# Routing stage of a two-layer block: unread products on TensorE, a merge in four column groups, exponentials kept in PSUM

## The reference, cut to what matters

```python
logits = jnp.einsum('bsd,ed->bse', x, gate_w) + gate_b      # x: 8 x 512 x 256, 32 experts
probs = jax.nn.softmax(logits, axis=-2)                      # over the 512 tokens
vals_t, idx_t = jax.lax.top_k(probs.transpose(0, 2, 1), K)   # K = 8
...
tok = jnp.take_along_axis(x, flat_idx[:, :, None], axis=1)
tok = tok.reshape(b, K, E, d)
merged = jnp.einsum('bked,bke->bed', tok, vals)              # 8 x 32 x 256
```

## Time and profile before

| | us |
|---|---|
| median of three runs | 1335.1 |
| the three runs | 1330.59, 1335.10, 1335.44 |
| the profiled execution | 1329.41 |
| its span in the trace | 1327.7 |
| PE busy | 1281.6 |
| DVE busy | 1050.0 |
| ACT busy | 948.6 |

### The profile page before, as it was taken

The page is one execution under the profiler, slowest core; times in us unless marked ns, Lnnn a source line. Parts: engine busy times, 40 slices in busy tenths (PEclk is TensorE's granted clock), DMA queues, the critical chain, the costliest instruction groups (busy, mean ns, idle before and its releaser), DMA issues. The chain is left out here.

```text
span 1327.7 us, 32264 instructions
## 1 busy us (share of the span) xinstructions
PE 1281.6 (97%) x11493; PEld 1068.5 (80%) x11493; DVE 1050.0 (79%) x3340; ACT 948.6 (71%) x2384; POOL 318.5 (24%) x694
## 2 busy tenths in 40 slices
PE   4799999999999999999999999999999789999999
PEld 3587788888878888888879788887978578888888
DVE  6968896989689689868986897798689757767673
ACT  5869895988589588858885986788598724444333
POOL 4533331322133222212331223133133100000000
PEclk9999999999999999999999999999999999999999
DMA  6552231323223232323323232233223222222100
GB/s 212 200 159 89 90 127 59 120 104 101 78 94 121 74 105 74 126 69 103 128 75 104 75 129 86 82 97 106 89 89 112 78 77 63 57 57 56 57 17 33
DMA packets 90831, 125.18 MB, mean 94 GB/s; under 512 B 8760, under 2 KB 77104, under 8 KB 90672
## 3 DMA queue, kind: packets, MB, share of 16 engines
q1 hardware_dynamic: 90352, 123.11, 28.6%
q10 hardware_dynamic: 320, 0.00, 0.0%
HBM read 103.69 MB, written 19.40 MB: 93 GB/s over the span
## 5 line engine op out<-in xcount | busy, mean ns | idle before, releaser
L1213 ACT ACTIVATE prob<-prob,low 128x512 f32<-128x512 f32 (+3 forms) x512 | 281.2, 552 | 107.1 <-DVE low L1376 107.1
L1376 DVE CUSTOM_DVE_ANT_0 prob<-at,mask 128x512 f32<-128x512 f32 (+3 forms) x512 | 219.7, 485 | 8.9 <-PE at L960 8.9
L947 PE MATMUL at<-w_hi,c_lo 128*128 128x386 f32 x512 | 187.9, 367 | 0.8 <-DVE area_raw L1321 0.8
L947 PE MATMUL at<-w_lo,c_hi 128*128 128x386 f32 x512 | 174.1, 340 | 0.0
L947 PE MATMUL at<-w_hi,c_hi 128*128 128x386 f32 x512 | 173.9, 340 | 0.0
L1389 DVE TENSOR_SCALAR prob<-prob,rec 128x512 f32<-128x512 f32 (+3 forms) x512 | 169.9, 395 | 4.5
L999 PE MATMUL at<-ident,prob 128*128 128x128 f32 x1280 | 165.9, 276 | 4.5 <-DVE low L1376 1.8
L1027 PE MATMUL at<-probT,v 128*32 128x512 f32 (+3 forms) x2048 | 152.7, 439 | 2.6 <-DVE probT L1399 2.6
L999 PEld LDWEIGHTS at<-ident,prob 128*128 128x128 f32 x1280 | 141.8, 140 | 14.8 <-issue 4.6
L1527 POOL TENSOR_TENSOR area_sq<-area_sq 128x512 f32<-128x512 f32 x64 | 82.3, 1287 | 249.7 <-ACT area_sq L1177 249.7
L1027 PEld LDWEIGHTS at<-probT,v 128*32 128x32 f32 x2048 | 60.7, 110 | 93.4 <-issue 82.5
(11 more groups left out here) (265 smaller groups left out, 3226.8 us busy)
## 6 DMA issues: line engine op xcount, KB each, us to landing
area_w<-in_L_ffn_w SPq DMA_DIRECT2D x65, 1024.0 KB, 5.6
bias<-in_L_ffn_w SPq DMA_DIRECT2D x160, 32.0 KB, 4.4
x_in<-in_L_attn_x SPq DMA_DIRECT2D x8, 512.0 KB, 5.5
xr<-in_L_attn_x SPq DMA_DIRECT2D x8, 512.0 KB, 4.7
eo_d<-hidT SPq DMA_DIRECT2D x32, 128.0 KB, 1.8
x_d<-xr SPq DMA_DIRECT2D x8, 512.0 KB, 2.8
area_raw<-x_d SPq DMA_DIRECT2D x8, 512.0 KB, 3.9
out<-area_raw SPq DMA_DIRECT2D x7, 512.0 KB, 3.0
```

What stands on the lines that cost most here:

```text
L947: m = eng.matmul(bQ[n % 2][:, 0:W], a[:, (j // HP) % 2, k, n * P:(n + 1) * P], w[:, k, j % HP, :], start=start, stop=(k == KC - 1 and a is ...
L1213: eng.activation(sl, sl, ACT.Exp, scale=-1.0, bias=low[:, i:i + 1], accum_out=den[:, i:i + 1]).then_inc(exp_done.sem, 1)
L1376: eng.tensor_tensor_reduce(out=prob[s % 2][h][:, off[c]:off[c + 1]], in0=bC[i][:, at:at + (c + 1) * P], in1=mask[:, (NT - 1 - c) * P:T], s ...
```

## The change

It has three parts.

1. *Unread products.* For b >= 2, `turn_x(b)` begins with two products of the unit matrix with itself, repeated over 512 columns, into the bank that the turned tokens then overwrite, and `gate(b)` with three products of 512 columns into the logits' rows, which the first real product then overwrites. Nobody reads the five.
2. *Merge.* The picks become the weights (128 x 32) and the tokens the moving operand (256 columns). The four token tiles go to four groups of 32 PE columns, and so to four groups of 32 PSUM partitions. These four partial sums are then copied to SBUF by DVE (`copy_part`, a new instruction) and added by two more products on PE (`add_parts`) with a 128 x 32 matrix `stack` of four unit matrices, made once at the start. `copy_merged` on ACT now waits for the second of them.
3. *Exponentials.* `expd` is no longer a tile in SBUF but partitions 32 to 63 of bank 6, beside the logits.

```diff
-    pe_xT, pe_gate, pe_pickT, pe_merged = ev("pe_xT", KC), ev("pe_gate", 1), ev("pe_pickT", 1), ev("pe_merged", 1)
+    pe_xT, pe_gate, pe_pickT, pe_merged = ev("pe_xT", KC), ev("pe_gate", 1), ev("pe_pickT", 1), ev("pe_merged", 2)
...
+    expd = bL[E:2 * E, :]
...
+        def keep_busy(out, weights, count):
+            for i in range(count):
+                eng.matmul(out, weights, unit[:, :].unsqueeze(1).to_broadcast([P, NT, P]), start=True, stop=True)
+
         def turn_x(b):
             eng.wait_ge(lo_done.sem, lo_done.at(b - 2))
+            if b >= 2:
+                keep_busy(bT[b % 2][0][:, :], unit[:, :], 2)
             eng.wait_ge(xn_done.sem, xn_done.at(b))
...
             eng.wait_ge(logits_done.sem, logits_done.at(b - 1))
+            if b >= 2:
+                keep_busy(bL[0:E, :], gT_hi[:, 0, :], 3)
...
+            for n in range(NT):
+                m = eng.matmul(bank_of(b)[n * E:(n + 1) * E, KC * E:KC * E + C], pickT_of(b)[:, n, :], xn[b % SLOTS][:, n, :],
+                               start=True, stop=True)
+            m.then_inc(pe_merged.sem, 1)
+
+        def add_parts(b):
+            eng.wait_ge(merged_done.sem, merged_done.at(b, 1))
             for k in range(KC):
-                for n in range(NT):
-                    m = eng.matmul(bank_of(b)[:, k * E:(k + 1) * E], xn[b % SLOTS][:, n, k * P:(k + 1) * P], pickT_of(b)[:, n, :],
-                                   start=(n == 0), stop=(n == NT - 1))
+                m = eng.matmul(bank_of(b)[:, k * E:(k + 1) * E], part[:, k * P:(k + 1) * P], stack[:, :], start=True, stop=True)
             m.then_inc(pe_merged.sem, 1)
...
+            if 0 < b < B - 1:
+                add_parts(b - 1)
             if b + 1 < B:
                 gate(b + 1)
...
         merge(B - 2)
+        add_parts(B - 2)
         merge(B - 1)
+        add_parts(B - 1)
...
+        def copy_part(b):
+            eng.wait_ge(pe_merged.sem, pe_merged.at(b, 1))
+            eng.tensor_copy(part[:, :], bank_of(b)[:, KC * E:KC * E + C]).then_inc(merged_done.sem, 1)
+
...
             if b + 1 < B:
                 split_low(b + 1)
+            if 0 < b < B - 1:
+                copy_part(b - 1)
...
+        copy_part(B - 2)
+        copy_part(B - 1)
```

More of the change, by code:

```diff
@@ L197, in routing_tiles @@
         ("nmax", [E, 1], F32),
-        ("expd", [E, T], F32),
         ("den", [E, 1], F32),
@@ L202, in routing_tiles @@
         ("pickT", [P, NT, E], F32),
+        ("part", [P, C], F32),
+        ("stack", [P, E], F32),
         ("raw_w", [P, KC, 3, H * D], F32),
@@ L219, in route_tokens @@
     B, T, C, NT, KC, E, H, D = (g[k] for k in ("B", "T", "C", "NT", "KC", "E", "H", "D"))
-    ident, merged, half = g["ident"], g["merged"], g["half"]
+    ident, unit, merged, half = g["ident"], g["unit"], g["merged"], g["half"]
     xnT_hi_d, xnT_lo_d, pick_d = g["xnT_hi_d"], g["xnT_lo_d"], g["pick_d"]
@@ L229, in route_tokens @@
     x, xn = [tiles[f"x_in{u}"] for u in range(SLOTS)], [tiles[f"xn_{u}"] for u in range(SLOTS)]
-    logits, top8, left, nmax, expd, den, rden, pick, pickT = (tiles[k] for k in (
-        "logits", "top8", "left", "nmax", "expd", "den", "rden", "pick", "pickT"))
+    logits, top8, left, nmax, den, rden, pick, pickT = (tiles[k] for k in (
+        "logits", "top8", "left", "nmax", "den", "rden", "pick", "pickT"))
     raw_w, u_in, u_blk, u_sq, u_half, tmp, ss, slope, om, e0, l0, gk, qk_w, qaug32 = (tiles[k] for k in (
@@ L238, in route_tokens @@
     bT, bL, bP, bM = (bank[2:4], bank[4:6]), bank[6], bank[7][:, 0:P], bank[7][:, P:]
+    expd = bL[E:2 * E, :]
+    part, stack = tiles["part"], tiles["stack"]
     ev = lambda name, per, unit=1: Signal(ctx, nc, "r_" + name, per, unit)
-    gate_load, gate_t, gate_copied = ev("gate_load", 2, 16), ev("gate_t", 1), ev("gate_copied", 2)
+    gate_load, gate_t, gate_copied = ev("gate_load", 2, 16), ev("gate_t", 1), ev("gate_copied", 3)
     load = [ev(f"load{u}", 1, 16) for u in range(SLOTS)]
@@ L249, in route_tokens @@
     kept_done, pick_done, merged_done, pickT_done = (
-        ev("kept_done", 1), ev("pick_done", 1), ev("merged_done", 1), ev("pickT_done", 1))
-    pe_xT, pe_gate, pe_pickT, pe_merged = ev("pe_xT", KC), ev("pe_gate", 1), ev("pe_pickT", 1), ev("pe_merged", 1)
+        ev("kept_done", 1), ev("pick_done", 1), ev("merged_done", 2), ev("pickT_done", 1))
+    pe_xT, pe_gate, pe_pickT, pe_merged = ev("pe_xT", KC), ev("pe_gate", 1), ev("pe_pickT", 1), ev("pe_merged", 2)
     logits_done, exp_done, w_hi_done, w_lo_done = ev("logits_done", 1), ev("exp_done", 1), ev("w_hi_done", 1), ev("w_lo_done", 1)
@@ L426, in norm @@
             eng.wait_ge(shift_done.sem, shift_done.at(b))
-            eng.wait_ge(pe_merged.sem, pe_merged.at(b - SLOTS))
+            eng.wait_ge(pe_merged.sem, pe_merged.at(b - SLOTS, 1))
             for n in range(NT):
@@ L450, in exp @@
             eng.wait_ge(pick_done.sem, pick_done.at(b - 1))
-            eng.activation(expd[:, :], logits[:, b % 2, :], ACT.Exp, bias=nmax[:, 0:1],
+            eng.activation(expd, logits[:, b % 2, :], ACT.Exp, bias=nmax[:, 0:1],
                            accum_out=den[:, 0:1]).then_inc(exp_done.sem, 1)
@@ L455, in copy_pick @@
             if b < B - 1:
-                eng.wait_ge(pe_merged.sem, pe_merged.at(b - 1))
+                eng.wait_ge(pe_merged.sem, pe_merged.at(b - 1, 1))
             else:
@@ L591, in weigh @@
             eng.wait_ge(left_done.sem, left_done.at(b))
-            eng.scalar_tensor_tensor(left[:, :], left[:, :], LOWEST / 2, expd[:, :],
+            eng.scalar_tensor_tensor(left[:, :], left[:, :], LOWEST / 2, expd,
                                      ALU.is_le, ALU.mult).then_inc(kept_done.sem, 1)
@@ L649, in finish_omega @@
             eng.tensor_copy(qaug[:, :], qaug32[:, :]).then_inc(ready.sem, 1)
+        eng.tensor_reduce(stack[:, :], ident.rearrange("p (j e) -> p e j", e=E), AX.X, ALU.add).then_inc(gate_copied.sem, 1)
         moments(0)
@@ L654, in vector @@
         eng.tensor_copy(gT_hi[:, :, :], grid).then_inc(gate_copied.sem, 1)
-        eng.wait_ge(gate_copied.sem, gate_copied.at(0, 1))
+        eng.wait_ge(gate_copied.sem, gate_copied.at(0, 2))
         eng.tensor_tensor(gT_lo[:, :, :], grid, gT_hi[:, :, :].bitcast(F32), ALU.subtract).then_inc(gate_copied.sem, 1)
```

## The result

The changed kernel takes 1342.8 us (median of four runs, 1342.67 to 1343.44). The kernel before took 1332.9 beside it (four runs, 1330.59 to 1335.44). The ratio is 1.0081, 95% interval 1.0060 to 1.0102: slower by 0.8%. In three later measurements, with 19 to 31 runs each, the kernel before had medians of 1330.6, 1330.6 and 1332.3, so the loss is between 10 and 12 us. The profiled execution took 1343.44 us, with a span of 1341.4, against 1329.41 and 1327.7 before: 14.0 us more. That is more than the medians differ by, since the profiled execution of before was one of its quickest.

The account below looks back on a forecast made before the run. DVE was taken to bound the routing (6.81 us a turn), ACT close second. Terms 5.0 + 1.4 + 2.0 + 0.8 + 1.6 = +10.8 us took the profiled 1329.4 to 1340.2; allowing for slower runs, 1344, range 1336 to 1352.

Parts of the forecast that it names:

- the ring: Routing turn: MAX, low parts, `copy_part`, `add_parts`, `copy_merged`, `norm`, weights, logits, MAX take 8.05 us, not 6.81; chance 0.58.
- Item 1: Turns 1 to 4 of the routing: each takes 8.05 us instead of 6.81, together +5.0 us.
- Item 2: Turn 5: `finish_gate_keys` comes late and POOL's last `w_lo` catches one of its instructions before MAX, +1.4 us.
- item 3: Turn 6: `copy_part`, `add_parts` and three unread products put the gate's first product 4.3 us behind MAX, +2.0 us.
- item 4: Turn 6: PE idles some 4 us and the half clock comes earlier; between 0 and +1.7, taken as +0.8 us.
- Item 5: End of the routing: DVE does two `copy_part` before `mean_square`, on the chain to `turn_q`, +1.6 us.
- One to one into the end: From routing to kernel end: a routing delay goes through in full, since the attention behind is bound by PE.
- 1344: Whole kernel: the forecast median in us, from 1340.2 profiled, raised because the other runs of before were slower.
- A: Routing: POOL's `w_lo` also holds `nmax`, turns 2 to 5 each losing up to 0.9 us; +15 us, 1348; chance 0.15.
- B: Turn 6 and routing end: unread products hold 2.4 GHz, key columns slip in before POOL; +7 us, 1340; chance 0.16.
- C: Routing: ACT isn't held, turns stay bound by DVE and shrink by 0.55 us; faster, some 7 us, 1328; chance 0.04.
- D: Whole kernel: the attention's first steps give the delay back, or savings and ring cancel; 1335; chance 0.07.

Follow-up runs that it names:

- e4: The changed kernel with `copy_merged` moved behind `norm` in ACT's queue; 1336.6 us, ratio 1.0035 to the kernel before.
- e13: The changed kernel with `copy_part` moved ahead of `split_low` on DVE; 1333.5 us, ratio 1.0011 to the kernel before.
- e8: The changed kernel with the gate's three unread products moved ahead of `add_parts`, into PE's wait; 1338.8 us, ratio 1.0055 to the kernel before.
- e5: The changed kernel without the five unread products; 1339.7 us, ratio 1.0067 to the kernel before.
- e9: The changed kernel with the old merge for batches 6 and 7; 1340.3 us, ratio 1.0054 to the kernel before.
- e1: The kernel before with only the exponentials moved to PSUM; 1331.8 us, ratio 1.0003 to the kernel before.
- e2: The kernel before with only the five unread products added; 1329.3 us, ratio 0.9977 to the kernel before.
- e3: The changed kernel without unread products and with `expd` in SBUF, leaving only the new merge; 1338.5 us, ratio 1.0051 to the kernel before.
- e10: The changed kernel with `copy_merged` behind `norm`, `add_parts` behind the gate, `finish_gate_keys` behind turn 6's low parts, old merge for batches 5 to 7; 1325.5 us, ratio 0.9946.
- e6: The changed kernel with `copy_merged` behind `norm`, `add_parts` behind the gate, old merge for batches 6 and 7; 1330.1 us, ratio 0.9988 to the kernel before.
- e7: The same as e6 but without the unread products; 1330.5 us, ratio 0.9991 to the kernel before.

## The prediction against the runs

**The direction and the ring: right.** Turns 3 and 4 took 8.13 and 8.12 for a forecast of 8.05. ACT's wait before `copy_merged` was 2.11 for 2.0. The single prices: the product 0.68 (forecast 0.75), `copy_part` 0.41 (0.40), `merge` 0.64 (0.64), `add_parts` 0.46 to the next instruction (0.5), three unread products 0.70 to the next (0.7), all in turn 3 and at the whole clock. e4 and e13 show the ring by breaking it in two different places.

**Item 1, turns 1 to 4: +6.0 for a forecast of +5.0.** The mechanism was right, the size was off by the clock. Turn 2 took 8.99. Behind a wait of 2.54 us in turn 1 PE went to 1.2 GHz between 30 and 31 us (granted clock 0.50 from 31 to 37), and the rows there are:

```profile
35.47 0.60 ACT L459 ACTIVATE xT_hi<-at 128x512 fp32r<-128x512 f32 x1 [1.41 <-PE at L365]
```

```profile
29.04 0.63 PE L406 MATMUL at<-stack,part 128*128 128x32 f32 x4 [2.54 <-DVE part L610]
...
33.36 1.22 PE L356 MATMUL at<-ident 128*128 128x512 f32 x2
```

The two unread products ahead of the turned tokens took 1.22 us instead of 0.73, the turning behind them 1.91 instead of 1.09 (both as e8 has them at the whole clock), and ACT waited 1.41 us for it. The ring passes over PE there, and my sum had the half clock only in turn 6. In e5 the turning is at 1.2 GHz as well (1.97 us), but the two products ahead of it are gone, and turn 2 takes 8.0; so it does in e8, with three of them in the wait. A second such stretch, about 48 to 51 us, cost turn 4 nothing: ACT waited 0.73 us for the turned tokens and then less for `add_parts` (1.26), and the turn took 8.12.

**Item 2, turn 5: +1.5 for +1.4.** MAX6 came 9.45 us behind MAX5 (forecast 9.3), and the instruction that POOL caught is the second CAST of the keys, 2.06 us. e5 and e8 confirm the path: without three unread products between `add_parts` and the turned keys nothing is caught, though by 0.2 us only in both.

**Items 3 and 4, turn 6: +4.0 for +2.8.** PE's wait was 3.89 us (forecast some 4). The gate's first product came 5.22 us behind the MAX, forecast 4.3 and before 2.26: +3.0 for +2.0. From there to MAX7 it is 5.20 us for 4.16 before: +1.0. All six products of the gate were at 0.63. Ahead of them `add_parts` took 0.87 us to the next instruction, not 0.5, and the three unread products 1.26, not 0.7: both were at 1.2 GHz already. At the whole clock that part would have been 4.3, so item 3 stands, and the whole surplus belongs to item 4, the clock. It comes to 0.9 us ahead of the gate and 1.0 behind it, less 0.3 that MAX7 to `merge(6)` is shorter, since six projections lie at the half clock in place of ten: +1.7, twice the +0.8 that I took, and the upper end of my own range of 0 to +1.7. I had counted the slow clock for the gate and `keep_busy` there (+1.8) but not for `add_parts`, and then took a middle value without a row for it.

**Item 5, the end: +1.7 for +1.6** from `merge(6)` to `turn_q`, and e9 gives 1.8. One wait wasn't foreseen: `add_parts(7)` stood 1.81 us for ACT's `copy_merged(6)`, which is behind the reciprocal root in ACT's queue. It cost nothing, since `turn_q` had to wait for DVE longer than that.

**One to one into the end: right here.** +12.6 at `turn_q`, +13.7 in the span. Other traces are less exact: between steps 58 and 63 the delay rises by 1.2 us in e1, e2, e9 and e13, and falls by 1.5 to 1.6 in e3 and e4. So the end of a single trace is good to 1.5 us or so.

**The number 1344 is nearer than its sum.** From the profiled execution I had worked out 1340.2, and it took 1343.4: the sum was 3.2 us short. Of these 1.8 were there at `turn_q`, mostly by the clock in turns 2 and 6, and the rest came behind it, where I had nothing: 0.4 to step 0, 0.6 in the attention, the remainder after it. To this I added 3.3 us, since the other runs of before were slower than its profiled one. The changed kernel's four runs lie within 0.8 us of each other, so this addition didn't apply. Two errors of 3 us cancelled, and that the number came so near is luck. The spread of the kernel before is real, and it goes with the granted clock: in the later measurements fifteen runs at 0.994 have a mean of 1329.4 us, nine at 0.986 one of 1334.8.

**Rivals.** A, POOL holding `nmax`: false. In turns 3 to 5 `nmax` lay within `w_lo` (43.64 within 42.81 to 44.99) and took 0.14 us. The lock that the Trainium skill states ("SBUF — State Buffer", Who interferes with whom) and that `tensor_scalar` can enter didn't show there. It agrees with the product (1.70 us with two SBUF inputs, 0.68 with one) and with the CAST of turn 5. B, less of it because the unread products hold the clock: false as placed. The rule of the Trainium skill ("TensorE: Matmul & The Clock Gate", What's actually happening), that idleness throttles, does agree with the 3.89 us wait ahead of the half clock here, and with e2, where the wait is filled and the clock stays. The length of the last wait alone doesn't tell when it falls: in turn 6 e13 waits 2.70 us and stays at 1.00, and the kernel before waited 2.02 us and fell. C, that ACT isn't held: false by 2.11 us of wait, but true of e10, which has the other order. D, nothing: false.

## What to carry to other kernels

An instruction that became shorter isn't a gain if the change adds a round trip between engines: count the ring that the new waits close, engine by engine, and put the new step where its input is ready, and behind those things that others wait for. Work whose only purpose is to keep PE's clock belongs ahead of the wait that it is to fill. Behind it, it costs its duration on everything that waits, and it held the clock only in part here (0.85 against 0.75 without and 0.95 in the wait). And when an engine idles more in a stage, price the stretch at the half clock for everything that follows the idle time, the new instructions among it.

## What the runs showed of the chip that I had not expected

- POOL's 128 x 1024 `w_lo` holds some small DVE instructions and not others. The CAST of 128 x 16 in SBUF took 2.06 us inside it, 0.18 outside. The TENSOR_SCALAR of 32 x 1 in SBUF took 0.14 us inside it. The product of 32 x 512 took 0.68 with one operand in PSUM, 1.70 with both in SBUF beside `w_lo`, and 0.66 with both in SBUF where no `w_lo` runs. Whether it is the operation or the size that spares `nmax` wasn't tried.
- The same five unread products lowered the time by 1.4 us in e2, raised it by 3.1 (changed kernel against e5), and did nothing in e6 against e7. The kernels around them differ too; e8, where only their place does, moved the time by 4.1 us.
- A gain at the end of the routing doesn't always reach the end of the kernel. e1 had 2.5 us at `turn_q` and e2 1.3, and in step 0 of the attention 1.5 and none were left, with more half clock in the stretch behind (0.85 and 0.83 from 76 to 96 us, for 0.91 before). Losses reached step 0 in full (e3, e4 and the changed kernel), and so did 4.7 of the 4.8 us of e10, which has 0.96 there. Why the clock falls in one and not in the other stayed open.
